# A four-layer graph network on one core: layer two's pass over all nodes dropped, its rows finished in the pass over edges

## The chip, the cores and the metric

One core of a Trainium2 chip runs the whole program, one launch. The metric is the device time in microseconds (us) of that core; a run's time takes in the program's span and what lies around it. Engine names are those of the profile: PE (TensorE), DVE (VectorE), ACT (ScalarE), POOL (GpSimd), SP (the queue that issues most transfers).

## The reference, cut to what matters

50,000 nodes with 256 features, 25,000 edges sorted by destination `dst`. Four layers, each followed by a layer norm over the features; all in float32.

```python
x = _layernorm(x + _L0_gnn_ref(...))   # messages, matmul, batch norm, relu, matmul
x = _layernorm(x + _L1_gnn_ref(...))   # x, mean of edge features, u -> hidden 512 -> 256
x = _layernorm(x + _L2_gnn_ref(x, src, dst, L2_gnn_W, L2_gnn_attn_l, L2_gnn_attn_r))
x = _layernorm(x + _L3_gnn_ref(x, edge_index, L3_gnn_W, ...))

def _L2_gnn_ref(feat, src, dst, W, attn_l, attn_r):          # 8 heads of 32
    ft = (feat @ W).reshape(n, H, D)
    a1, a2 = einsum('nhd,hd->nh', ft, attn_l), einsum('nhd,hd->nh', ft, attn_r)
    e = leaky_relu(a1[src] + a2[dst], 0.2)
    ex = exp(e - segment_max(e, dst)[dst])
    alpha = ex / segment_sum(ex, dst)[dst]
    return elu(segment_sum(ft[src] * alpha, dst))

def _L3_gnn_ref(...):   # 4 heads of 64; the same attention, with a self-loop for each node
    ...
    return elu(out + bias) + x
```

A node that is no edge's destination gets a zero sum in layer two, so that its new row is the layer norm of its old row, which is normed already: the old row times one factor. At most 25,000 of the 50,000 nodes are a destination.

## The kernel before

Seven stages run one after the other, with a barrier between them (`barrier`, the `tick` memset at L234). `PHASES` lists five programs for each stage, one for each engine. Each engine runs its instructions in the order in which the code writes them; semaphores tie them together.

- **Stage 1** (`p1_*`) sums the messages of the edges into `tab0` and prepares weights and indices. **Stage 2** (`p2_*`) is the first matmul of layer nought over all nodes, with the statistics of the batch norm.
- **Stage 3** (`p3_*`, "the layer-one pass") takes 98 steps of 512 nodes (`NS = 98`, `J = 4` rows of each of 128 partitions). A step k: PE runs `hidden(k)` (L1044, L1048), `mmA(k+2)` (L1024), then the transposes of k+1 (L1031, L1038) between the four groups of `mmB(k)` (L1067). ACT runs `relu(k)` (L959: four instructions, each frees a bank of PSUM), `evac(k+1)`, `y(k+3)`. DVE runs `first(k+2)` and `second(k)`: sum, statistics and, after POOL's power (L794), the scaling at L799, twice for each step. POOL runs `lnA.rstd(k+2)`, `lnB.rstd(k)`, `xb(k+3)` (L891), `x1_b(k+2)` (L897), and four indirect stores of step k-1 (L917). `mmA(k+3)` and `mmB(k+1)` wait for the whole of `relu(k+1)`, since its last bank is shared and its rows are the operand:

```python
if BA + j // 2 == HB[KH - 1]:
    wait(pe, p3["hidr"], KH * (k.s - 1))
```

- **Stage 4** (`edge_pass(2, ...)`, "layer two's edge pass") takes 49 steps of 512 edges. POOL gathers the source rows (L1181, four of a step) and scatters finished rows to `tab` (L1192, four). PE transposes and multiplies, DVE runs the segmented maximum and sum as scans, then for each of four tiles the recurrence L1387, L1391 and the division L1402.
- **Stage 5** (`node_pass`, "layer two's node pass") reads `tab` and `x2_d` for all nodes, takes the elu, the sum and the layer norm, stores `x3_d`, multiplies by layer three's weights and stores `h3_d` and the attention terms `ad_d`.
- **Stage 6** (`edge_pass(3, ...)`) does for layer three what stage 4 does for two, on rows of `h3_d` that need no matmul.
- **Stage 7** (`last_pass`) reads `tab`, `h3_d` and `x3_d` for all nodes: POOL multiplies two sets of rows (L1819), PE adds them, ACT and DVE take the elu and the norm.

## Time and profile before

| what | value |
|---|---|
| runs (3) | 5734.33, 5746.14, 5750.26 us; median 5746.14 |
| span of the profiled execution | 5581.5 us |
| busy in it: PE / DVE / ACT / POOL | 4162.6 / 3702.1 / 1962.3 / 3611.4 us |
| moved over HBM | 627.40 MB read, 543.83 MB written |

The profile shows one execution's span, from the first to the last instruction of the program; of that execution only the span is given. The runs' times are longer than a span, since they take in what lies around it: 5746.14 - 5581.5 = 164.6 us between the median and this span.

### The profile page before, as it was taken

What the parts mean: (1) busy time and instruction counts of PE and PEld (TensorE: products, weight loads), DVE (VectorE), ACT (ScalarE), POOL (GpSimd) and SP (SyncE); (2) the same over time, 40 slices, a digit from 0 to 9 for tenths busy, and PEclk for the clock granted to TensorE, in tenths of its full rate; (3) what the DMA queues carried; (4) which work ended last, traced back from release to release, by engine and by line L of the source; (5) the groups of instructions that cost most, each with busy time, mean ns of one, the idle gap of its engine ahead of it and who ended that gap; (6) DMA issues with size and microseconds to landing.
All of it is one profiled execution on the core that took longest, in us unless ns stands there. A gap on an engine that the chain in (4) does not pass through costs nothing. (4 is left out here: it accounts for less than half of the span.)

```text
span 5581.5 us, 69994 instructions
## 1 busy us (share of the span) xinstructions
PE 4162.6 (75%) x16758; PEld 2810.8 (50%) x16758; DVE 3702.1 (66%) x10203; ACT 1962.3 (35%) x3345; POOL 3611.4 (65%) x3319
## 2 busy tenths in 40 slices
PE   2276679999999999999999977776877500036666
PEld 1154445556666666666666667665666400012222
DVE  2155456666666666666666667777999665568887
ACT  0011135532222222222222222226888400026666
POOL 7488654443555556555555567775888777768887
PEclk7689889999999999999999988887999855569988
DMA  9988789985433333333333244447999733359998
GB/s 376 294 153 156 148 263 366 364 329 186 149 124 120 119 127 123 120 117 124 122 117 116 84 133 138 138 136 255 351 348 351 248 95 94 95 181 343 357 344 289
DMA packets 497175, 1129.62 MB, mean 202 GB/s; under 512 B 164007, under 2 KB 246907, under 8 KB 497031
## 3 DMA queue, kind: packets, MB, share of 16 engines
q1 hardware_dynamic: 331530, 866.20, 44.4%
q0 software_dynamic: 113184, 174.84, 12.9%
q10 hardware_dynamic: 52316, 87.06, 4.5%
q8 instruction: 41, 0.67, 0.0%
q14 instruction: 104, 0.84, 0.0%
HBM read 627.40 MB, written 543.83 MB: 210 GB/s over the span
## 5 line engine op out<-in xcount | busy, mean ns | idle before, releaser
L1067 PE MATMUL psum<-W2b,arena 128*128 128x256 f32 x3136 | 725.4, 380 | 0.0
L799 DVE TENSOR_SCALAR arena<-arena 128x256 f32<-128x256 f32 x784 | 462.6, 651 | 366.3 <-POOL arena L794 361.8
L1048 PE MATMUL psum<-arena,W1b 128*128 128x512 f32 x1568 | 699.2, 599 | 0.0
L1067 PEld LDWEIGHTS psum<-W2b,arena 128*128 128x128 f32 x3136 | 574.6, 191 | 65.2 <-issue 0.5
L1761 PE MATMUL psum<-arena,ident 128*128 128x512 f32 x784 | 409.9, 672 | 208.1 <-POOL arena L1819 206.0
L959 ACT ACTIVATE arena<-psum,hbias 128x512 f32<-128x512 f32 x392 | 269.4, 687 | 821.2 <-PE psum L1048 821.2
L1048 PEld LDWEIGHTS psum<-arena,W1b 128*128 128x128 f32 x1568 | 290.6, 190 | 401.7 <-issue 401.7
L1192 POOL DMA_INDIRECT tab<-arena,IDX x392 | 405.1, 1033 | 122.8 <-issue 91.5
L790 POOL TENSOR_TENSOR arena<-arena,lneps 128x4 f32<-128x4 f32 x196 | 41.5, 212 | 670.1 <-DVE arena L786 669.1
L1610 POOL DMA_INDIRECT ad_d<-arena,FE x392 | 394.6, 1007 | 114.3 <-issue 113.7
L917 POOL DMA_INDIRECT xd_d<-arena,FE x360 | 378.1, 1050 | 99.8 <-issue 96.9
L440 POOL DMA_INDIRECT tab<-arena x196 | 310.6, 1585 | 165.7 <-DMA tab<-zero 65.3
L1251 PE MATMUL psum<-ident,arena 128*128 128x128 f32 x24 | 5.8, 434 | 528.0 <-DVE arena L1419 516.8
L1555 PE MATMUL psum<-Wg,arena 128*128 128x264 f32 x1568 | 382.6, 400 | 19.2 <-DVE arena L1629 19.2
L1761 PEld LDWEIGHTS psum<-arena,ident 128*128 128x128 f32 x784 | 159.3, 213 | 458.0 <-issue 404.5
L1819 POOL TENSOR_TENSOR arena<-arena 128x1024 f32<-128x1024 f32 x196 | 368.3, 1900 | 10.4 <-DVE arena L1872 7.7
L1024 PE MATMUL psum<-W2a,arena 128*128 128x256 f32 x1568 | 356.9, 381 | 9.3 <-ACT arena L945 9.3
L752 PE MATMUL psum<-arena,W1a 128*128 128x512 f32 x784 | 353.7, 595 | 0.0
L702 POOL DMA_INDIRECT fe_d<-EID,FIRST x196 | 198.9, 1015 | 235.5 <-ACT arena L727 198.5
L1024 PEld LDWEIGHTS psum<-W2a,arena 128*128 128x128 f32 x1568 | 300.3, 192 | 91.6 <-issue 54.2
L1555 PEld LDWEIGHTS psum<-Wg,arena 128*128 128x128 f32 x1568 | 301.5, 197 | 76.2 <-DVE arena L1629 26.3
L577 PE MATMUL psum<-arena,NEG 128*128 128x324 f32 x500 | 161.2, 484 | 232.8 <-ACT arena L388 200.3
(256 smaller groups left out, 9286.1 us busy)
## 6 DMA issues: line engine op xcount, KB each, us to landing
arena<-tab SPq DMA_DIRECT2D x194, 544.0 KB
arena<-x_d SPq DMA_DIRECT2D x202, 512.0 KB, 7.0
arena<-in_x SPq DMA_DIRECT2D x194, 512.0 KB, 4.8
x_d<-arena SPq DMA_DIRECT2D x194, 512.0 KB, 2.9
tab<-zero SPq DMA_DIRECT2D x11, 5832.0 KB, 54.9
tab<-blank SPq DMA_DIRECT2D x97, 544.0 KB
h_d<-arena SPq DMA_DIRECT2D x97, 528.0 KB, 6.0
arena<-h_d SPq DMA_DIRECT2D x97, 528.0 KB, 5.5
```

Of the source, the lines that this page charges most:

```text
L440: pool.indirect_dma_start(out=tab0[:, :], out_offset=bass.IndirectOffsetOnAxis(ap=sidx[:, s, j:j + 1], axis=0), in_=comb[:, s % NC, j, :], ...
L752: last = pe.matmul(psum[:, 4 + 2 * b + g, :], W1a[:, f, g * P:(g + 1) * P], hT[:, b, f, :], start=(f == 0), stop=(f == FH - 1))
L799: v.tensor_scalar(y[:, j, :], r[:, j, :], self.mv[:, j, 0:1], self.rs[:, j:j + 1], ALU.subtract, ALU.mult).then_inc(self.s["y"], 1)
L917: pool.indirect_dma_start(out=xd_d[:, :], out_offset=bass.IndirectOffsetOnAxis(ap=FE[:, s * J + j:s * J + j + 1], axis=0), in_=x2[:, s % 2 ...
L1024: last = pe.matmul(outA(j), p3y[:, f, j * P:(j + 1) * P], W2a[:, f, :], start=(f == 0), stop=(f == FH - 1))
L1048: last = pe.matmul(psum[:, HB[c], :], W1b[:, f, c * P:(c + 1) * P], x1T[:, f, :], start=False, stop=(f == FH - 1))
L1067: last = pe.matmul(outB(j), hid[:, c, j * P:(j + 1) * P], W2b[:, c, :], start=(c == 0), stop=(c == KH - 1))
L1192: pool.indirect_dma_start(out=tab[:, :], out_offset=bass.IndirectOffsetOnAxis(ap=IDX[:, 2, c:c + 1], axis=0), in_=fin[:, s % NG, j, :], in ...
L1555: last = pe.matmul(psum[:, 2 + j, 0:HW], xT[:, k.slot(2), f, j * P:(j + 1) * P], Wg[3][:, f, :], start=(f == 0), stop=(f == FH - 1))
L1610: pool.indirect_dma_start(out=ad_d[:, :], out_offset=bass.IndirectOffsetOnAxis(ap=FE[:, c:c + 1], axis=0), in_=hs[:, k.slot(NB), j, D + H3 ...
L1761: last = pe.matmul(psum[:, b + i, :], ident[:, :], a[:, k.slot(2), 2 * i:2 * i + 2, :].rearrange("p j d -> p (j d)"), start=(n == 0), stop ...
L1819: pool.tensor_tensor(out=a[:, b, :, :].rearrange("p j (h c) -> p j h c", h=H), in0=t[:, k.slot(NB), :, 0:D].rearrange("p j (h c) -> p j h ...
```

## The change

Stage 5 is dropped, and its work is put in four other places.

- **Stage 3** writes `x3_d` for every node as if it were no destination: POOL takes one more power a step (`lone_pow`), ACT one more scaling of the step's rows (`lone_rows`), DVE three small instructions, SP one more store of 512 KB.
- **Stage 4** (`e2_*`) finishes the destination rows. The coefficients are divided once by the sum, so that the recurrence gives finished rows and L1402 goes. ACT takes relu and exp of a step's rows (`relu_exp`), DVE the elu (`settle`), POOL adds the destination's old rows (`residual`), DVE takes the statistics behind the next step's row sums (`measured`), POOL the power (`rstd`), ACT scales (`normed`), POOL scatters to `x3_d`. Two plain stores a step keep the unfinished and the finished rows in edge order (`raw_d`, `xl_d`). DVE copies the old row along a segment (one more 256-wide instruction for each tile).
- **Stage 6** (`e3_*`) goes through the edges from the last to the first, gathers rows of `x3_d`, and multiplies them itself, as stage 4 does. The self-loop's term is one more in its scans. DVE adds the bias (`biased`).
- **Stage 7** (`l_*`) reads `tab` and `x3_d`, and multiplies the rows by layer three's weights itself. DVE multiplies the product by the self-loop's share, POOL adds the edges' part (`total`) and the old rows (`residual`).

The core of the diff:

```diff
@@ p3_gpsimd @@
+            def lone_pow(k):
+                pool.wait_ge(lonely["lvar"], 3 * (k.s + 1))
+                wait(pool, lonely["lrow"], J * (k.s - 1))
+                pool.tensor_tensor(out=lonec[:, k.b, :], in0=lonev[:, k.b, :], in1=expo[:, 0:J], op=ALU.pow).then_inc(lonely["lpow"], 1)
             for s in range(NS):
...
                 if s + 2 < NS:
                     x1_b(at(s + 2))
+                if s > 0:
+                    lone_pow(at(s - 1))
@@ p3_scalar @@
+            def lone_rows(k):
+                act.wait_ge(lonely["lpow"], k.s + 1)
+                act.wait_ge(lnB.s["y"], J * (k.s + 1))
+                wait(act, p3_w3[k.b], 16 * k.n)
+                for j in range(J):
+                    act.activation(x3d[:, k.b, j, :], x2[:, k.b, j, :], ACT.Identity, bias=zero[:, 0:1], scale=lonec[:, k.b, j:j + 1]).then_inc(lonely["lrow"], 1)
...
                 if live(k.plus(3), NS):
                     y(k.plus(3))
-            run_steps(act, NS, body, tail=3)
+                if not (k.known() and k.s == 0):
+                    lone_rows(k.plus(-1))
+            run_steps(act, NS, body, peel=4, tail=3)
@@ e2_gpsimd @@
+            for s in range(CS + 2):
+                for j in range(J):
+                    if s + AHEAD < CS:
+                        gather(s + AHEAD, j)
+                    if s >= 2:
+                        scatter(s - 2, j)
+                    if j == 0 and 1 <= s <= CS:
+                        residual(s - 1)
+                    if j == J - 1 and 1 <= s <= CS:
+                        rstd(s - 1, ve2, neg2, rs2[:, (s - 1) % 2, :], nm2[:, (s - 1) % 2, :], J * (s - 2))
@@ e2_scalar @@
+            for s in range(CS):
+                ex(s)
+                if s + 1 < CS:
+                    for j in range(J):
+                        ev(s + 1, j)
+                if s > 0:
+                    normed(s - 1)
+                tail(s)
+                wait(act, e2["S"], J * (s + 1))
+                relu_exp(s, row2[:, s % NG, :, 0:D], un2, s)
@@ e2_vector @@
+            for s in range(CS):
+                chain(s)
+                if s > 0:
+                    settle(s - 1)
+                sums_rows(s)
+                if s > 0:
+                    measured(s - 1)
@@ l_gpsimd @@
+            def body(k):
+                total(k)
+                if not (k.known() and k.s < 1):
+                    residual(k.plus(-1))
+                if not (k.known() and k.s < 2):
+                    rstd(k.plus(-2))
@@ l_vector @@
+            def body(k):
+                weighted(k)
+                if not (k.known() and k.s < 1):
+                    unit(k.plus(-1))
+                if not (k.known() and k.s < 2):
+                    stats(k.plus(-2))
-        PHASES.append(edge_pass(2, x2_d, H2))
-        PHASES.append(node_pass(x2_d, x3_d))
-        PHASES.append(edge_pass(3, h3_d, H3))
-        PHASES.append(last_pass(x3_d, out, H3))
+        PHASES.append((e2_sync, e2_scalar, e2_gpsimd, e2_vector, e2_tensor))
+        PHASES.append((e3_sync, e3_scalar, e3_gpsimd, e3_vector, e3_tensor))
+        PHASES.append((l_sync, l_scalar, l_gpsimd, l_vector, l_tensor))
```

How the instructions stand, with the semaphores that they wait for. First ACT in the layer-one pass, a step k near its end and the first of the next: `relu(k)`, `evac(k+1)`, `y(k+3)`, `relu(k+1)`, before

```order
L959 ACTIVATE arena<-psum,hbias 128x512 [waits p3_hidw,p3_mmB]
L959 ACTIVATE arena<-psum,hbias 128x512 [waits p3_hidw] x3
L951 ACTIVATE arena<-psum 128x512 [waits p3_tr] x2
L953 ACTIVATE arena<-psum 128x512 [waits p3_tr]
L945 ACTIVATE arena<-arena,bnB,bnA 128x512 [waits p3_mmA,p3_h1]
L945 ACTIVATE arena<-arena,bnB,bnA 128x512
L959 ACTIVATE arena<-psum,hbias 128x512 [waits p3_hidw,p3_mmB]
```

and with the change:

```order
L1006 ACTIVATE arena<-psum,hbias 128x512 [waits p3_hidw,p3_mmB]
L1006 ACTIVATE arena<-psum,hbias 128x512 [waits p3_hidw] x3
L998 ACTIVATE arena<-psum 128x512 [waits p3_tr] x2
L1000 ACTIVATE arena<-psum 128x512 [waits p3_tr]
L992 ACTIVATE arena<-arena,bnB,bnA 128x512 [waits p3_mmA,p3_h1]
L992 ACTIVATE arena<-arena,bnB,bnA 128x512
L1013 ACTIVATE arena<-arena,zero 128x256 [waits p3_w31,lnB_y,p3_lpow]
L1013 ACTIVATE arena<-arena,zero 128x256 x3
L1006 ACTIVATE arena<-psum,hbias 128x512 [waits p3_hidw,p3_mmB]
```

The scaling of step k-1's rows (L1013), which waits for POOL's `lone_pow(k-1)` (semaphore p3_lpow), now stands between `y(k+3)` and `relu(k+1)`.

Then POOL in the same pass: the powers of k+2 (lnA) and k (lnB), `xb(k+3)`, `x1_b(k+2)`, the stores of k-1, before

```order
L790 TENSOR_TENSOR arena<-arena,lneps 128x4 [waits lnA_mv]
L794 TENSOR_TENSOR arena<-arena,expo 128x4 [waits lnA_ve,lnA_y]
L790 TENSOR_TENSOR arena<-arena,lneps 128x4 [waits lnB_mv]
L794 TENSOR_TENSOR arena<-arena,expo 128x4 [waits lnB_ve,lnB_y]
L891 TENSOR_TENSOR arena<-arena,b2a 128x1024 [waits p3_x0]
L897 TENSOR_TENSOR arena<-arena,b2b 128x1024 [waits lnB_y,lnA_y]
L917 DMA xd_d<-arena,FE 25088x256 [waits lnB_y]
```

and with the change:

```order
L813 TENSOR_TENSOR arena<-arena,lneps 128x4 [waits lnA_mv]
L817 TENSOR_TENSOR arena<-arena,expo 128x4 [waits lnA_ve,lnA_y]
L813 TENSOR_TENSOR arena<-arena,lneps 128x4 [waits lnB_mv]
L817 TENSOR_TENSOR arena<-arena,expo 128x4 [waits lnB_ve,lnB_y]
L930 TENSOR_TENSOR arena<-arena,b2a 128x1024 [waits p3_x0]
L936 TENSOR_TENSOR arena<-arena,b2b 128x1024 [waits lnB_y,lnA_y]
L962 TENSOR_TENSOR arena<-arena,expo 128x4 [waits p3_lrow,p3_lvar]
L956 DMA xd_d<-arena,FE 25088x256 [waits lnB_y]
```

The new power of step k-1 (L962, p3_lpow's source) stands behind the power of step k and both additions.

Last ACT in layer two's edge pass, one step s, before

```order
L1274 ACTIVATE arena<-arena 128x16x4 [waits g_S,g_d]
L1269 ACTIVATE arena<-psum 128x512 [waits g_mm,g_tr]
L1281 ACTIVATE arena<-arena 128x2x4x8 [waits g_s3,g_s]
L1269 ACTIVATE arena<-psum 128x512 [waits g_mm,g_tr] x3
L1274 ACTIVATE arena<-arena 128x16x4 [waits g_S,g_d]
```

and with the change:

```order
L1412 ACTIVATE arena<-arena 128x16x4 [waits e2_cf,e2_d]
L1407 ACTIVATE arena<-psum 128x512 [waits p2_mm,p2_tr] x4
L1431 ACTIVATE arena<-arena 128x256 [waits s_xd1,table_in1,e2_nm]
L1431 ACTIVATE arena<-arena 128x256 x3
L1417 ACTIVATE arena<-arena 128x2x4x8 [waits rows_out2,e2_s]
L1422 ACTIVATE arena<-arena 128x1024 [waits e2_u,e2_S]
L1424 ACTIVATE arena<-arena 128x1024 [waits e2_mn]
```

Between one step's exp (L1412, semaphore e2_d) and the next now stand `normed(s-1)` (L1431, which waits for POOL's `rstd(s-1)`, semaphore e2_nm) and `relu_exp(s)` (L1422, L1424, which wait for DVE's rows of step s, e2_S).

## Rows read from the trace of the kernel before

**Rows 1.** Windows, one for each of the seven stages, in order of time:

```profile
core 0 of [0], span 5581.5 us
core 0: us, PE busy (x) PEld busy (x) DVE busy (x) ACT busy (x) POOL busy (x), PEclk, DMA share, GB/s
0.00:745.00 745.00, 383.88 (x1386) 270.38 (x1386) 293.54 (x1032) 74.24 (x203) 505.75 (x414) 0.79 0.86 216
745.00:1183.00 438.00, 425.97 (x1568) 232.14 (x1568) 260.03 (x305) 241.04 (x392) 199.94 (x199) 0.98 0.98 352
1183.00:3232.00 2049.00, 2028.10 (x8232) 1370.70 (x8232) 1362.45 (x3237) 582.57 (x882) 1109.60 (x982) 1.00 0.39 133
3232.00:3798.00 566.00, 425.12 (x2408) 382.87 (x2408) 407.83 (x1493) 140.01 (x297) 413.04 (x397) 0.82 0.43 134
3798.00:4434.00 636.00, 482.97 (x2352) 389.46 (x2352) 553.31 (x1470) 489.83 (x784) 487.65 (x441) 0.94 0.95 327
4434.00:4954.00 520.00, 6.74 (x28) 5.98 (x28) 300.99 (x1049) 29.68 (x150) 391.10 (x397) 0.50 0.33 102
4954.00:5581.00 627.00, 409.86 (x784) 159.26 (x784) 523.91 (x1617) 404.90 (x637) 504.37 (x492) 0.90 0.92 328
```

**Rows 2.** Timeline of PE, one step of the layer-one pass and the next's start:

```profile
...
2711.18 1.99 PE L1044 MATMUL psum<-arena,W1e 64*128 64x512 f32 x8
...
2720.07 3.62 PE L1024 MATMUL psum<-W2a,arena 128*128 128x256 f32 x16
...
2731.84 1.99 PE L1044 MATMUL psum<-arena,W1e 64*128 64x512 f32 x8
...
```

**Rows 3.** Timeline of ACT, the same step:

```profile
...
2735.78 0.69 ACT L959 ACTIVATE arena<-psum,hbias 128x512 f32<-128x512 f32 x1 [5.29 <-PE psum L1048]
...
```

**Rows 4.** Timeline of POOL, the same step:

```profile
...
2735.32 1.01 POOL L794 TENSOR_TENSOR arena<-arena,expo 128x4 f32<-128x4 f32 x1 [0.44 <-POOL arena L790]
...
2739.90 2.35 POOL L897 TENSOR_TENSOR arena<-arena,b2b 128x1024 f32<-128x1024 f32 x1 [1.26 <-DVE arena L799]
```

**Rows 5.** Timeline of DVE, the same step:

```profile
...
2736.36 3.40 DVE L799 TENSOR_SCALAR arena<-arena 128x256 f32<-128x256 f32 x4 [1.76 <-POOL arena L794]
...
```

**Rows 6.** DVE's product at L982: engine, count, duration ns min/median/max, first and last:

```profile
...
L982 DVE TENSOR_TENSOR arena<-arena x98: 693/2624/2725, 1189.8 to 3173.6; 128x512 f32<-128x512 f32 x98
...
```

**Rows 7.** Windows in layer two's edge pass, columns as in rows 1:

```profile
...
3455.80:3459.20 3.40, 0.00 (x0) 0.00 (x0) 3.26 (x10) 0.00 (x0) 2.48 (x4) 0.89 0.72 244
3459.30:3465.20 5.90, 5.90 (x20) 5.18 (x21) 2.47 (x17) 1.45 (x3) 4.66 (x5) 0.50 0.30 91
...
```

**Rows 8.** Groups by form, layer two's edge pass: busy us, mean ns | idle:

```profile
...
L1192 POOL DMA_INDIRECT tab<-arena,IDX x196 | 208.0, 1061 | 63.0 <-issue 56.1 <-ACT arena L1269 3.5 <-DVE arena L1402 1.8
...
```

**Rows 9.** Timeline of DVE, one step of layer two's edge pass:

```profile
...
3453.30 0.24 DVE L1320 TENSOR_TENSOR_SCAN arena<-arena 128x40 f32<-128x40 f32 x1 [0.32 <-ACT arena L1274]
...
3455.12 0.36 DVE L1387 TENSOR_TENSOR arena<-arena 128x256 f32<-128x256 f32 x1
...
3457.11 0.42 DVE L1387 TENSOR_TENSOR arena<-arena 128x256 f32<-128x256 f32 x1
...
3458.27 0.41 DVE L1387 TENSOR_TENSOR arena<-arena 128x256 f32<-128x256 f32 x1
...
```

**Rows 10.** Groups by form, last pass, columns as in rows 8:

```profile
...
L1819 POOL TENSOR_TENSOR arena<-arena 128x1024 f32<-128x1024 f32 x196 | 368.3, 1900 | 10.4 <-DVE arena L1872 7.7 <-PE psum L1761 2.7
L1787 ACT ACTIVATE arena<-arena 128x256 f32<-128x256 f32 x392 | 201.8, 585 | 2.9 <-POOL arena L1831 2.4 <-ACT arena L1787 0.5
L1890 DVE BATCH_NORM_STATS2 arena<-arena 128x6 f32<-128x256 f32 x392 | 137.7, 413 | 5.5
L1882 DVE SCALAR_TENSOR_TENSOR psum<-arena,psum 128x1024 f32<-128x1024 f32 x98 | 120.0, 1225 | 15.6 <-ACT arena L1780 10.6 <-issue 5.0
...
L1780 ACT ACTIVATE arena<-arena 128x1024 f32<-128x1024 f32 x98 | 103.6, 1057 | 3.1
...
L1894 DVE BATCH_NORM_AGGREGATE arena<-arena 128x2 f32<-128x6 f32 x392 | 36.6, 156 | 4.3
...
```

More of the change, by code:

```diff
@@ L821, in gnn_program @@
         p3_w = [sem(f"p3_w{b}") for b in range(2)]
+        p3_w3 = [sem(f"p3_w3{b}") for b in range(2)]
+        lonely = {k: sem(f"p3_{k}") for k in ("lvar", "lpow", "lrow")}
         p3_fill = sem("p3_fill")
@@ L878, in body @@
                     store(k.plus(-4))
+                if not (k.known() and k.s < 5):
+                    store3(k.plus(-5))
                 if k.known() and 12 <= k.s < 12 + LATE:
@@ L1091, in gnn_program @@
         PHASES.append((p3_sync, p3_scalar, p3_gpsimd, p3_vector, p3_tensor))
-        once = {k: sem(f"g_{k}") for k in ("zero", "end", "old", "spread", "top", "z2", "wx", "f0", "wT", "new", "fr", "row", "fix", "near")}
-        edge2 = {k: sem(f"g_{k}") for k in
-                 ("tr", "ev", "mm", "chain", "eL", "M", "d", "w", "s", "tail", "A", "B", "S", "head", "inv", "full")}
         NG = 4
-        gs = [sem(f"g_g{b}") for b in range(NG)]
-        sc = [sem(f"g_s{b}") for b in range(NG)]
@@ new lines, in gnn_program @@
+        zb2 = take([H2, P])
+        wT2 = take([H2, P])
+        mx2 = take([H2])
+        df2 = take([2, H2])
+        wf2 = take([2, H2])
+        sn2 = take([H2])
+        pick = take([P])
+        same0 = take([C])
+        few = take([6])
+        e2 = {k: Signal(sem(f"e2_{k}")) for k in
+              ("tab", "rowd", "zero", "head", "hrow", "ev", "chain", "eL", "M", "d", "w", "s", "tail", "cf", "B", "A", "S", "xc",
+               "mn", "ex", "u", "r", "nm", "end", "spread", "top", "wx", "wT", "old", "z", "wf", "new", "fix", "fixed")}
@@ new lines, in gnn_program @@
+        ws3 = take([2, H3, J + 1])
+        inv3 = take([H3, J])
+        cf3 = take([2, 2, H3, J + 1])
+        om3 = take([2, H3, J + 1])
+        endrow3 = take([TW])
+        oldrow3 = take([TW])
+        newrow3 = take([TW])
+        tO3 = take([TW])
+        zb3 = take([H3, P])
+        wT3 = take([H3, P])
+        mx3 = take([H3])
+        df3 = take([2, H3])
+        wf3 = take([2, H3])
+        sn3 = take([H3])
+        e3_end = cursor[0]
+        done2 = dict(zero=5, head=16, tr=J * CS, ev=J * CS, mm=J * CS, chain=CHAIN * CS, eL=3 * CS, M=2 * CS, d=2 * CS, w=CS, s=CS, tail=CS,
+                     cf=3 * CS, B=2 * CS, A=J * CS, S=J * CS, end=2, spread=3, top=3, wx=1, wT=1, old=16, z=2, wf=1, new=13, fix=1, fixed=32)
@@ new lines, in gnn_program, with l_rows, l_sync, tables @@
+        l_w = [e2_xl[b].after(16 * turns(b)) for b in range(NG)]
+        def l_rows(sp, k):
+            b = k.slot(NXT)
+            wait(sp, lp["r"], k.s - NXT + 1)
+            a, n = node_view(x3_d, k)
+            sp.dma_start(l_xt[0:n, b, :, :], a).then_inc(l_x[b].sem, 16)
+        def l_sync(sp):
+            def tables(k):
+                b = k.slot(NTT)
+                wait(sp, lp["t"], k.s - NTT + 1)
+                a, n = node_view(tab, k)
+                sp.dma_start(l_tt[0:n, b, :, :], a).then_inc(l_t[b].sem, 16)
+            for s in range(NTT):
+                tables(beat(s, PER))
+            def body(k):
+                if live(k.plus(NTT), NS):
+                    tables(k.plus(NTT))
+                if not (k.known() and k.s == 0) and live(k.plus(NXT - 1), NS):
+                    l_rows(sp, k.plus(NXT - 1))
+            run_beats(sp, NS, body, PER, tail=NXT)
+            for b in range(4):
+                wait(sp, l_w[b], 16 * ((NS + 3 - b) // 4))
```

1667 lines of the change are left out of this document (898 added, 769 removed).

## The prediction

> **What bounds the kernel now.** First the windows, one for each stage [rows 1], since a mean over the span mixes seven different limits. The reader is to see three kinds. Stages 2 and 3 are PE's: 2028.1 of 2049 us busy in stage 3, at a granted clock of 1.00. Stages 5 and 7 are the transfers': DMA share 0.95 and 0.92 at 327 and 328 GB/s, with no engine over 90% busy. Stages 4 and 6 are POOL's: each of its indirect requests takes 1.061 us and 63.0 / 196 = 0.32 before the next [rows 8], so eight of a step take 11.0, and 49 steps 541 of the stage's 566 us. Then the timelines of one step of stage 3, one for each engine [rows 2 to 5]. A step lasts 2731.84 - 2711.18 = 20.66 us, and PE never stands; the other engines have slack, but their order within the step is tight, and that is where this change puts its new instructions.
>
> **Stage 5, dropped.** Its whole window goes: -636 us [rows 1]. Its transfers need not be made up elsewhere: the 51 MB of `x3_d` are now stored in stage 3 (98 steps of 512 KB), where the DMA share is 0.39.
>
> **Stage 3: one factor and one scaling a step.** By busy time this is free: ACT is busy 582.6 of 2049 us and POOL 1109.6 [rows 1]. By order it is not. `lone_rows(k-1)` stands on ACT ahead of `relu(k+1)`, and waits for `lone_pow(k-1)`, which stands on POOL behind `x1_b(k+2)`. That in turn waits for DVE's scaling in `second(k)`, which comes after `mmB(k)`. So `relu(k+1)`, due at 2735.78 [rows 3], falls behind all of these. Step by step, with `mmB(k)` ending at 2731.84 [rows 2]:
> DVE's scaling ends at 2736.36 + 3.40 = 2739.8 [rows 5], and about 0.4 later with three small instructions between (my estimate, below the 0.24 each of a scan over 40 columns [rows 9]): 2740.2. `x1_b` takes 2.35 [rows 4]: 2742.6. The power takes 1.01 [rows 4] and a signal: 2743.7. Four scalings of 256 columns at 0.585 [rows 10]: 2746.0. Four relus at 0.69 [rows 3]: 2748.8. Only now may PE take the second half of `mmA(k+3)`, 3.62 / 2 = 1.8 us [rows 2], and then the transposes and `mmB(k+1)`, which last 2731.84 - (2720.07 + 3.62) = 8.15 [rows 2]: 2758.8. From one end of `mmB` to the next that is 27.0 us, 6.3 more than 20.66, and it is a closed loop: the next step starts with the same delay. PE stands from the half of `mmA`, 2740.7 + 1.8 = 2742.5, to 2748.8, in one piece.
>
> Such a standstill has a second price. In stage 4 PE stood for the 3.4 us from 3455.8, and then worked for 5.9 us without a gap at a granted clock of 0.50, the lower level of 1.2 GHz [rows 7]. If the 6.3 us do the same, the work behind them begins at 1.2 GHz, and it is all on the loop. Bounds: nothing, or 3.0 us, half of those 5.9; I take 2.3, since part of the low stretch falls into the standstill. The Trainium skill ("TensorE: Matmul & The Clock Gate", Part 1) says that the throttled state is the default and that activity releases it, with no third level between; by that rule the clock falls in each step, and the trace agrees, with 0.50 and 1.00.
> So a step takes 27.0 + 2.3 = 29.3, and 96 steps have both neighbours: 96 x 8.6 = **+826 us** (bounds 96 x 6.3 = 605 and 96 x 9.3 = 893).
>
> **Stage 4: rows finished.** Again the order decides, not the sum. Let DVE's row sums of step s end at 0. `measured(s-1)`: four statistics and four aggregates, 4 x 0.413 + 4 x 0.156 [rows 10], 2.3. POOL's power and product, 1.01 [rows 4] and 0.2 (estimate): 3.5. ACT's `normed(s-1)`, 4 x 0.585 [rows 10]: 5.8; its copy of the sums, 0.3 (estimate): 6.1; `relu_exp(s)`, 2 x 1.057 [rows 10]: 8.3. DVE, which has long done `chain(s+1)`, has waited for that; `settle(s)` takes what L1882 takes, 1.22 [rows 10]: 9.5. Then `sums_rows(s+1)`: from the scan to the first row product it is 3455.12 - 3453.30 = 1.8 now [rows 9], and 2.3 with the two small products more; for each tile three 256-wide instructions, as now (the old row's copy where the division was), 3458.27 - 3457.11 = 1.16 [rows 9], so 4.6.
> Between them comes a new collision: POOL adds the destination rows, 1024 columns from two tiles of SBUF, just when DVE has small products with two operands there. The row to read is L982: 0.693 us at the least, 2.624 at the median [rows 6], and in each step `x1_b` runs at that moment (2739.90 to 2742.25 [rows 4]). So DVE's product waits for POOL's addition to end. I take 2.35 as its length, since it is an addition of the same shape as `x1_b`; the other bound is the 1.90 of L1819 [rows 10], a product with a broadcast. Of the 2.3 us of small work at most the scan and the reciprocal run beside it or before it (0.35, an estimate): +2.0. The loop is 9.5 + 2.3 + 4.6 + 2.0 = 18.4 us; without the collision and with the short addition 16.4; with the six requests between `residual` and `rstd` at 1.38 each as the longer way, up to 19.5. The Trainium skill ("SBUF — State Buffer", "Who interferes with whom") has the rule for this: VectorE with two SBUF inputs and GpSimd reading SBUF exclude each other for a whole instruction. By it the loop is 18.4, without it 16.4, a difference of 98 us in the stage; rows 6 agree with it. For the addition's length only a page has a figure of the plain kind ("GPSIMD Engine Reference", 3.1): 4497 ns for 2048 columns, so an estimate of 2.25 for 1024, which would take 5 us off the stage.
> 49 x 18.4 = 902, and 40 for filling and for the last row's repair (now 566 - 541 = 25, plus one step's lag): 942 against 566, **+376 us** (bounds +278, +430).
>
> **Stage 6: its own matmul, backwards.** POOL's eight requests a step stay, and with them the stage's step now, 520 / 49 = 10.6 [rows 1]. DVE: stage 4's 407.8 / 49 = 8.3 now [rows 1], less four divisions (each a third of the 1.16 in rows 9, so 1.5), plus a bias addition of 1.2 [rows 10] and a dozen small ones (1.8, an estimate): 9.8. PE's part, absent now, needs a bank that DVE frees shortly before the row sums end, and may be late by 1 us at the lower clock (an estimate). I take 11.5: 49 x 11.5 + 30 = 594, **+74 us** (bounds 10.6 and 12.5 a step: +29, +123).
>
> **Stage 7: a quarter fewer bytes.** 512 + 544 + 512 KB in place of 2096 a step: at 328 GB/s [rows 1] 4.9 us, so the transfers no longer bind (6.4 a step now). POOL does: two additions of 1024 columns, 2 x 2.35, and 1.2 for power and product, with gaps 6.1; and DVE's `unit`, 1.22, also reads two SBUF tiles, so that it excludes the additions: 7.3 if it never falls beside the power, 6.1 if always. I take 6.7: 98 x 6.7 + 15 = 672 against 627, **+45 us** (bounds 5.3, with additions of 1.90 and no exclusion, so -90; 7.3, so +104). Stages 1 and 2 keep their work but for a few instructions (0 us).
>
> **Sum.** -636 + 826 + 376 + 74 + 45 = +685 on the profiled span: 5581.5 + 685 = 6266. The median of the runs is 164.6 above that span, and what lies around a span does not change: 6431, so 6430 us.
>
> **Rivals.**
> - *The standstill without the clock's fall.* For: in stages 5 and 7 PE stands 1.6 and 2.2 us in each of 98 steps, and the clock is still 0.94 and 0.90 [rows 1]. Against: rows 7. 6430 - 96 x 2.3 = 6209. Chance 0.17.
> - *Stage 4 keeps to POOL's own pace*, 11.0 + 2.35 + 1.2 = 14.6 a step, the other engines' loop being shorter than I read it. For: POOL binds there now. Against: the loop has each link in the code. 6430 - 49 x 3.8 = 6244. Chance 0.08.
> - *The scaled rows do hide in stage 3* (the other side). For: ACT and POOL have over 900 us each to spare there. Against: the order of rows 4 and 3, with `relu(k+1)` due at 2735.78 and `x1_b` beginning at 2739.90. 6430 - 826 = 5604, faster. It decides where the delay is below 1.5 us a step, since the rest sums to -141 us and 141 / 96 = 1.5. Chance 0.10.
> - *Nothing to tell*: gains and losses cancel to within 0.3% (17 us, about what a measurement here can tell). Chance 0.03.
> - My forecast, with both prices in stage 3: 0.62, its own range 6250 to 6640.
>
> Slower is 0.62 + 0.17 + 0.08 = 0.87. All low bounds together give 5930 and all high ones 6660; they are independent, so I take 6050 to 6640, which holds the first two rivals and leaves out the third, the fourth and the corners.
>
> **What would show it.** In stage 3: steps of 27 to 29 us in place of 20.66, PE idle once a step for about 6 us before L1024's counterpart or the relus' reader, released by ACT; ACT's `lone_rows` released by POOL's power; a granted clock below 0.9. In stage 4: DVE idle ahead of `settle`, released by ACT's exp, about 3.5 us a step, and a median near 2 us for the coefficient product. In stage 7: DMA share near 0.75 and POOL over 85% busy. I am wrong if `x1_b(k+2)` runs ahead of the scaling of step k, or if stage 3 stays near 2049 us.

## The result, and the profile after

The changed kernel takes 6399.28 us, median of 4 runs (6394.61 to 6409.17), the kernel before 5746.53 in the same comparison: ratio 1.1137, 95% interval 1.1119 to 1.1154. That is 653 us more; the prediction said 6430, within 6050 to 6640. The number is right to 0.5%, but it is a sum in which two errors of some 165 us cancel (a stage mis-sized, and a difference between two executions taken for a constant); they are taken apart below.

The windows of the changed kernel, one for each stage in order of time (stage 5 is gone, so these are stages 1, 2, 3, 4, 6, 7), to be read against [rows 1]:

```profile
core 0: us, PE busy (x) PEld busy (x) DVE busy (x) ACT busy (x) POOL busy (x), PEclk, DMA share, GB/s
0.00:745.50 745.50, 406.39 (x1386) 280.62 (x1386) 292.95 (x1032) 73.91 (x203) 506.15 (x414) 0.76 0.86 215
745.50:1187.10 441.60, 426.47 (x1568) 231.73 (x1568) 259.87 (x305) 240.71 (x392) 199.21 (x200) 0.98 0.98 349
1187.10:4014.50 2827.40, 2277.32 (x8232) 1520.56 (x8232) 1379.44 (x3531) 741.84 (x1274) 1222.12 (x1081) 0.89 0.33 114
4014.50:4944.10 929.60, 486.07 (x2410) 424.48 (x2410) 665.54 (x2163) 326.41 (x593) 595.86 (x547) 0.69 0.40 135
4944.10:5705.60 761.50, 481.57 (x2388) 423.69 (x2388) 436.69 (x1942) 128.37 (x297) 392.19 (x397) 0.73 0.32 102
5705.60:6385.20 679.60, 508.80 (x2352) 424.47 (x2352) 519.07 (x1274) 503.82 (x780) 650.82 (x394) 0.90 0.68 224
```

In stages 3, 4 and 6, which grew most, no engine is busy for more than 0.81 of the window and the DMA share is 0.40 or less: something waits for something, in each. Stage 3 alone is 778 us longer.

Stage 3 against [rows 2 to 4]: first ACT's timeline around one standstill (start, length, what, and in brackets the idle time before it and what ended it):

```profile
3109.24 2.07 ACT L1013 ACTIVATE arena<-arena,zero 128x256 f32<-128x256 f32 x4 [13.34 <-POOL arena L962]
3111.21 2.39 ACT L1006 ACTIVATE arena<-psum,hbias 128x512 f32<-128x512 f32 x4
```

POOL's timeline, just before it:

```profile
3105.35 2.35 POOL L936 TENSOR_TENSOR arena<-arena,b2b 128x1024 f32<-128x1024 f32 x1 [1.60 <-DVE arena L1075]
3107.66 1.46 POOL L962 TENSOR_TENSOR arena<-arena,expo 128x4 f32<-128x4 f32 x1
```

And PE's:

```profile
3106.13 1.89 PE L1094 MATMUL psum<-W2a,arena 128*128 128x256 f32 x8
3113.65 3.78 PE L1094 MATMUL psum<-W2a,arena 128*128 128x256 f32 x8 [5.63 <-ACT arena L1006]
```

This is the predicted loop link by link: DVE's scaling (L1075), `x1_b` (L936), the lone rows' power (L962), the lone rows (L1013), the relus (L1006), and only then PE. ACT has stood for 13.34 us before its lone rows. PE stands 5.63 us, and its second eight products last 3.78 us, twice the 1.89 of the first eight: the granted clock is 0.50 from 3113.65 to 3117.40, the lower of the clock's two levels, 1.2 GHz, after the standstill.

Stage 4, DVE and POOL in one step, against [rows 9]. Settle waits for the exponential; beside POOL's addition (L1311) DVE's product of 64 columns takes 1.94 us:

```profile
4517.85 1.22 DVE L1537 SCALAR_TENSOR_TENSOR arena<-arena 128x1024 f32<-128x1024 f32 x1 [4.21 <-ACT arena L1424]
...
4519.15 2.34 POOL L1311 TENSOR_TENSOR arena<-arena 128x1024 f32<-128x1024 f32 x1 [3.18 <-DVE arena L1537]
...
4519.64 1.94 DVE L1565 TENSOR_TENSOR arena<-arena 128x64 f32<-128x64 f32 x1
```

Stage 6, groups of instructions over the whole stage (count, busy us, mean ns, idle us before them and who ended it; "remote" stands where the profile shows no instruction behind the signal). This stage's loop I had not worked out:

```profile
L1761 PE MATMUL psum<-Wg,arena 128*128 128x260 f32 x784 | 287.5, 503 | 250.5 <-ACT arena L1798 250.5
L1721 POOL DMA_INDIRECT tab<-arena,IDX x196 | 198.2, 1011 | 288.1 <-DVE arena L1878 229.0 <-issue 58.8 <-ACT arena L1808 0.3
...
L1837 DVE SCALAR_TENSOR_TENSOR arena<-KEEP,psum 128x8 f32<-128x8 f32 x98 | 15.9, 163 | 288.3 <-remote 263.7 <-PE psum L1763 21.4 <-issue 3.3
...
L1803 ACT ACTIVATE arena<-arena 128x48 f32<-128x48 f32 x49 | 11.9, 243 | 337.4 <-DVE arena L1872 337.4
```

Every engine waits for another one: PE for ACT's copies, ACT for DVE's chain, POOL for DVE's biased rows, and DVE, at the second instruction of its chain, for PE's last products. Lines of one step from the timelines of DVE, ACT and PE, in order of time:

```profile
5311.96 0.16 DVE L1837 SCALAR_TENSOR_TENSOR arena<-KEEP,psum 128x8 f32<-128x8 f32 x1 [4.89 <-remote]
...
5314.17 0.24 ACT L1803 ACTIVATE arena<-arena 128x48 f32<-128x48 f32 x1 [7.14 <-DVE arena L1872]
5314.32 1.06 ACT L1798 ACTIVATE arena<-psum 128x512 f32<-128x512 f32 x2
5314.95 2.10 PE L1761 MATMUL psum<-Wg,arena 128*128 128x260 f32 x4 [5.30 <-ACT arena L1798]
...
5324.20 0.51 PE L1763 MATMUL psum<-Wg,arena 128*128 128x8 f32 x4
...
5327.50 0.17 DVE L1837 SCALAR_TENSOR_TENSOR arena<-KEEP,psum 128x8 f32<-128x8 f32 x1 [6.26 <-remote]
```

This is the stage's loop. In the mean over the steps it takes 2.2 us from DVE's L1837 to ACT's exponential (L1803), 0.8 from there to PE's first product, 9.1 for PE's four times 128 rows with their copies, and 2.6 from the end of PE's last record to DVE's next L1837: 14.7 us, 49 times 720 of the stage's 762.

### The profile page after: what moved, and what is told of

The parts are those of the page before. It is cut to its first block and busy times, and to the rows that moved or that the text cites. A ratio compares the mean times of both kernels' runs of the same rounds, so it can differ in the third digit from the quotient of the medians.

```text
span 6395.2 us, 70077 instructions
## 1 busy us (share of the span) xinstructions
PE 4586.6 (72%) x18336; PEld 3305.5 (52%) x18336; DVE 3553.6 (56%) x10247; ACT 2017.3 (32%) x3543; POOL 3566.4 (56%) x3029
## 5 line engine op out<-in xcount | busy, mean ns | idle before, releaser
L1094 PE MATMUL psum<-W2a,arena 128*128 128x256 f32 x1568 | 546.1, 510 | 534.2 <-ACT arena L1006 524.8
L1094 PEld LDWEIGHTS psum<-W2a,arena 128*128 128x128 f32 x1568 | 392.3, 258 | 686.2 <-ACT arena L1006 562.6
L1013 ACT ACTIVATE arena<-arena,zero 128x256 f32<-128x256 f32 x392 | 203.0, 588 | 1281.7 <-POOL arena L962 1281.7
L1044 DVE TENSOR_TENSOR arena<-psum,arena 128x512 f32<-128x512 f32 x196 | 134.5, 686 | 813.3 <-PE psum L1094 813.3
L1372 PE MATMUL psum<-Wg,arena 128*128 128x264 f32 x784 | 289.6, 506 | 385.3 <-ACT arena L1407 383.6
L2030 PE MATMUL psum<-Wg,arena 128*128 128x256 f32 x1568 | 423.1, 431 | 153.5 <-ACT arena L2048 153.5
L1761 PE MATMUL psum<-Wg,arena 128*128 128x260 f32 x784 | 287.5, 503 | 250.5 <-ACT arena L1798 250.5
L2030 PEld LDWEIGHTS psum<-Wg,arena 128*128 128x128 f32 x1568 | 331.6, 216 | 227.7 <-ACT arena L2048 154.5
L1372 PEld LDWEIGHTS psum<-Wg,arena 128*128 128x128 f32 x784 | 179.1, 253 | 422.5 <-ACT arena L1407 395.4
L1721 POOL DMA_INDIRECT tab<-arena,IDX x196 | 198.2, 1011 | 288.1 <-DVE arena L1878 229.0
L1761 PEld LDWEIGHTS psum<-Wg,arena 128*128 128x128 f32 x784 | 180.6, 255 | 286.1 <-ACT arena L1798 262.7
L936 POOL TENSOR_TENSOR arena<-arena,b2b 128x1024 f32<-128x1024 f32 x98 | 230.1, 2348 | 157.0 <-DVE arena L1075 154.0
```

The costliest lines, as they stand in the source:

```text
L936: pool.tensor_tensor(out=x1b[:, k.b, :, :], in0=x1[:, k.b, :, :], in1=b2b[:, :].rearrange("p (a d) -> p a d", a=1).to_broadcast([P, J, D]) ...
L1013: act.activation(x3d[:, k.b, j, :], x2[:, k.b, j, :], ACT.Identity, bias=zero[:, 0:1], scale=lonec[:, k.b, j:j + 1]).then_inc(lonely["lrow ...
L1094: last = pe.matmul(outA(j), p3y[:, f, j * P:(j + 1) * P], W2a[:, f, :], start=(f == 0), stop=(f == FH - 1))
L1372: pe.matmul(o[:, 0:D + H2], xT2[:, j % 2, f, :], Wg[2][:, f, 0:D + H2], start=(f == 0), stop=(f == FH - 1))
L1721: pool.indirect_dma_start(out=tab[:, :], out_offset=bass.IndirectOffsetOnAxis(ap=IDX[:, 3, c:c + 1], axis=0), in_=fin3[:, s % NG, i, :], i ...
L1761: pe.matmul(o[:, 0:D + H3], xT3[:, i % 2, f, :], Wg[3][:, f, 0:D + H3], start=(f == 0), stop=(f == FH - 1))
```

## The experiments

Stage lengths below are read between the barrier's marks, each from one profiled execution; "us" is the median of four or more runs, but of one run for `e0_before` and `e10_tensor_less`. The kernel before was timed beside each.

| run | us | stage 3 | 4 | 5 | 6 | 7 |
|---|---|---|---|---|---|---|
| before, first profile | 5746.53, its runs | 2049 | 566 | 637 | 520 | 619 |
| before, second profile (`e0_before`) | 5762.88 | 2048 | 630 | 667 | 594 | 626 |
| changed | 6399.28 | 2827 | 930 | - | 762 | 680 |
| `e1_pow_first` | 5648.22 | 2063 | 938 | - | 766 | 680 |
| `e2_ev_first` | 6367.15 | 2825 | 929 | - | 736 | 679 |
| `e3_exp_first` | 6282.64 | 2828 | 811 | - | 767 | 680 |
| `e13_stats_first` | 6373.80 | 2827 | 907 | - | 759 | 680 |
| `e9_tiny_loads` | 6403.77 | 2830 | 929 | - | 765 | 679 |
| `e5_exp_dve_adds` | 6206.64 | 2838 | 731 | - | 759 | 680 |
| `e6_all_orders` | 5485.31 | 2063 | 811 | - | 734 | 682 |
| `e8_orders_dve` | 5513.47 | 2071 | 732 | - | 726 | 794 |
| `e11_orders_dve4` | 5411.70 | 2069 | 730 | - | 742 | 679 |
| `e10_tensor_less` | 5315.20 | 2067 | 732 | - | 640 | 682 |
| `e12_scatter_later` | 5298.84 | 2066 | 731 | - | 618 | 681 |

**What the profile of before was.**

> The kernel before, unchanged, profiled a second time. The changed kernel's run is 2.5 us longer than its span (6397.69 against 6395.2); before's profiled span lies 164.6 us under the median of its runs. Theory: nothing of 165 us lies around a span; before's profiled execution was itself some 160 us shorter than its other runs. Then this run's span is 2 to 3 us under its own time, and that time is either again near 5584 or near 5746; in the second case some stage of it is longer than in the first profile, and says which (744.5, 438.8, 2048.7, 565.6, 636.7, 519.7, 618.6 us there). Rival, as the prediction had it: the span is again near 5582 and the time near 5746.

Its span is 5761.2 us, under a time of 5762.88: nothing of 165 us lies around a span, and the first profile showed an execution quicker than any timed run. Stages 1 to 3 agree to 3 us; stages 4, 5, 6 and 7 are 65, 30, 74 and 8 longer. The windows of stages 4, 5 and 6 in the second profile, against [rows 1]:

```profile
3234.90:3865.30 630.40, 467.70 (x2408) 409.33 (x2408) 408.92 (x1493) 136.53 (x297) 405.14 (x396) 0.78 0.38 120
3865.30:4532.40 667.10, 493.01 (x2352) 395.66 (x2352) 551.54 (x1470) 492.87 (x784) 484.39 (x442) 0.93 0.90 312
4532.40:5126.10 593.70, 6.74 (x28) 5.99 (x28) 305.69 (x1049) 29.70 (x150) 391.09 (x397) 0.50 0.29 89
```

DVE's, ACT's and POOL's busy times are those of the first profile within 3%, so what grew is mostly waiting; PE is busy 43 us longer in stage 4, at a granted clock of 0.78 for 0.82. One place of stage 6 shows which waiting. DVE's timeline in the second profile:

```profile
4803.03 0.18 DVE L1352 TENSOR_TENSOR arena<-arena 128x16 f32<-128x16 f32 x1 [3.30 <-remote]
4804.43 0.18 DVE L1354 SCALAR_TENSOR_TENSOR arena<-arena 128x16 f32<-128x16 f32 x1 [1.22 <-DVE arena L1352]
4805.83 0.20 DVE L1320 TENSOR_TENSOR_SCAN arena<-NEG,arena 128x20 f32<-128x20 f32 x1 [1.22 <-DVE arena L1354]
4807.23 0.18 DVE L1359 TENSOR_TENSOR arena<-arena 128x16 f32<-128x16 f32 x1 [1.20 <-DVE arena L1320]
```

The same four operations in the first profile, DVE's timeline:

```profile
4700.64 0.18 DVE L1352 TENSOR_TENSOR arena<-arena 128x16 f32<-128x16 f32 x1 [3.87 <-DMA arena<-h_d,IDX]
4700.85 0.17 DVE L1354 SCALAR_TENSOR_TENSOR arena<-arena 128x16 f32<-128x16 f32 x1
4701.06 0.20 DVE L1320 TENSOR_TENSOR_SCAN arena<-NEG,arena 128x20 f32<-128x20 f32 x1
4701.30 0.17 DVE L1359 TENSOR_TENSOR arena<-arena 128x16 f32<-128x16 f32 x1
```

Each operation waits for the semaphore of the one just ahead of it on its own engine. In the first profile the signal is there at once, in the second it takes 1.2 us here. Over stage 6, such waits of DVE for itself alone are over 0.3 us in 69 of 301 cases, 76 us together, and never in the first profile (0.06 us at the most): about the 74 us by which the stage is longer. In stage 4 PE's signals are late. ACT's copies there, first profile, then second:

```profile
L1269 ACT ACTIVATE arena<-psum 128x512 f32<-128x512 f32 x196 | 116.7, 596 | 370.5 <-PE psum L1226 369.4
L1269 ACT ACTIVATE arena<-psum 128x512 f32<-128x512 f32 x196 | 113.2, 596 | 452.9 <-remote 152.3 <-PE psum L1226 139.0 <-PE psum L1237 84.4
```

Counted from the end of PE's records that a copy waits for (or of ACT's own last instruction, if that is later), 55 of 195 copies start over 0.5 us late, 188 us together; in the first profile none does. The 30 us of stage 5, where the transfers fall from 327 to 312 GB/s, are not traced to anything. So signals came late in stages 4 and 6, and the timed runs of before, at 5734 to 5770 us, are as long as this second execution. Why they are late is open; a candidate is the recording itself, though the first execution was recorded too. The second trace holds 49,859 semaphore updates where the first holds 80,775. The Trainium skill ("NOTIFIC — the notification-queue block", 7.1) says that the block that takes the records never loses one inside but holds its producers up; no run here tested that.

**Stage 3: order or work.**

```diff
             for s in range(NS):
+                if s > 0:
+                    lone_pow(at(s - 1))
                 if s + 2 < NS:
                     lnA.rstd(pool, at(s + 2))
...
-                if s > 0:
-                    lone_pow(at(s - 1))
                 if LATE < s < NS - 1:
```

> The changed kernel with one edit: GpSimd does the lone rows' power of step s-1 first in its pass s, ahead of both root steps, instead of last, behind the rows' add. Nothing is left out. Theory (stage 3's loss is ScalarE waiting with the lone rows for a power that GpSimd does behind work which itself waits for this step's VectorE, so a wait that closes a loop, and not work): stage 3 falls from 2827 to about 2050 to 2130 us, ScalarE's wait at the lone rows from 13.3 us a step to under 3, the granted clock there from 0.89 to near 0.99; the whole falls by some 700 to 780 us, to about 5620 to 5700 us. Rival (the step is longer by its added work: 2.07 us of ScalarE, 1.02 of GpSimd, VectorE's small products and the added store): the order is worth little and stage 3 stays over 2650 us.

```profile
1185.20:3247.70 2062.50, 2029.24 (x8232) 1368.22 (x8232) 1367.72 (x3531) 763.02 (x1274) 1211.65 (x1081) 1.00 0.47 157
```

5648.22 us, 0.9827 of before (0.9806 to 0.9848): one instruction in another place is worth 751 us, and the kernel is 1.7% faster than before in place of 11% slower. PE is busy as before the change, at a clock of 1.00, and all the added work of the lone rows costs 14 us. One number was off: ACT still waits 409.4 / 98 = 4.2 us at the lone rows, not under 3, but nothing is late behind it.

**Stage 4: the order on ACT, and who adds.**

```diff
-                if s > 0:
-                    normed(s - 1)
                 tail(s)
                 wait(act, e2["S"], J * (s + 1))
                 relu_exp(s, row2[:, s % NG, :, 0:D], un2, s)
+                if s > 0:
+                    normed(s - 1)
```

> The changed kernel with one edit in stage 4 (layer two's edge pass): ScalarE does the relu and the exponential of rows s ahead of the normed rows s-1, instead of behind them. Nothing is left out. Theory (the loop of stage 4 is VectorE's statistics s-1, GpSimd's power, ScalarE's normed rows s-1, relu and exponential s, VectorE's settle s, its row sums, statistics s): VectorE's wait of 4.0 to 4.2 us at settle goes, the step falls from 17.94 to 13.7 to 14.5 us, stage 4 from 930 to 720 to 780 us. Rival (GpSimd's add locks VectorE out and GpSimd's own 11.5 us a step with its waits set the pace): VectorE's wait moves to GpSimd's sum and the step stays over 16.5 us.

811 us, from 930: the wait at settle is gone, as the theory had it, but the stage is 31 us above the theory's range, at 15.4 us a step, between the theory and its rival. DVE, now without a gap there, runs into POOL's addition with its next operation, the scan of the row sums. That group in `e3_exp_first`:

```profile
L1195 DVE TENSOR_TENSOR_SCAN arena<-arena 128x40 f32<-128x40 f32 x49 | 121.0, 2470 | 40.8 <-ACT arena L1412 40.8
```

The next run keeps this edit and takes the addition away from POOL (its `residual` goes, DVE does the same behind settle):

```diff
             def settle(s):
...
+                wait(v, e2["u"], s + 1)
+                wait(v, e2["xc"], J * s + J - 1)
+                v.tensor_tensor(out=rr2[:, b, :, :], in0=xd2[:, c, :, :], in1=rr2[:, b, :, :], op=ALU.add).then_inc(e2["r"].sem, 1)
```

> The kernel of e3_exp_first with one more edit in stage 4: the destination rows are added by VectorE right behind its settle, and not by GpSimd. Nothing is left out. Behind e3_exp_first VectorE is busy nearly without a gap, and its small scan beside GpSimd's add of 2.37 us takes 2.74 us in place of 0.23. Theory (VectorE sets the pace there, and GpSimd's add costs it 2.5 us a step by holding it up, against some 1.2 us for doing the add itself): stage 4 falls from 811 to 725 to 760 us, the small operation behind settle is back under 0.4 us. Rival (moving work onto the engine that sets the pace costs it what the add takes, 1.2 to 2.4 us a step): stage 4 rises to 850 us or more.

731 us, as the theory had it. DVE does the addition in 1.23 us, and its scan is back at 274 ns:

```profile
L1538 DVE TENSOR_TENSOR arena<-arena 128x1024 f32<-128x1024 f32 x49 | 60.0, 1225 | 1.7
...
L1195 DVE TENSOR_TENSOR_SCAN arena<-arena 128x40 f32<-128x40 f32 x49 | 13.4, 274 | 0.3 <-issue 0.3
```

The change also puts the statistics behind the row sums. That part undone, with DVE's `measured(s - 1)` ahead of `sums_rows(s)`:

```diff
                     settle(s - 1)
+                    measured(s - 1)
                 sums_rows(s)
-                if s > 0:
-                    measured(s - 1)
```

> The changed kernel with one edit in stage 4: VectorE takes the statistics of rows s-1 ahead of the row sums of tile s, where the change puts them behind. Nothing is left out. Theory (in the changed kernel statistics, power, normed rows, relu, exponential and settle form one loop of 17.94 us a step; ahead of the row sums they run beside them): VectorE waits some 3 us for GpSimd's add and saves the 4.2 us at settle and 1.7 us of the held-up product; the step falls to 15.5 to 17 us, stage 4 from 930 to 800 to 880 us. Rival (the wait for GpSimd's add comes on top, the wait at settle stays): 20 us or more a step, stage 4 over 1000 us.

907 us, 22 less: the right sign, and too small for the theory; the rival's 1000 is far off. The timeline of one step, DVE and POOL, shows why:

```profile
4504.65 1.23 DVE L1537 SCALAR_TENSOR_TENSOR arena<-arena 128x1024 f32<-128x1024 f32 x1 [3.05 <-ACT arena L1424]
...
4508.33 1.40 DVE L1544 BATCH_NORM_STATS2 arena<-arena 128x6 f32<-128x256 f32 x4 [2.46 <-POOL arena L1311]
...
4510.26 0.16 DVE L1553 TENSOR_SCALAR arena<-arena 128x4 f32<-128x4 f32 x1
...
4516.21 1.23 POOL L1316 TENSOR_TENSOR arena<-arena,expo 128x4 f32<-128x4 f32 x1
```

The statistics are ready at 4510.42, but POOL takes their power at 4516.21, behind its six requests. Settle still waits, 3.05 us here. The loop keeps its links and only changes the one that is late.

**Stage 6: copies, loads, TensorE, requests.**

```diff
             for s in range(CS):
+                if s + 1 < CS:
+                    for i in range(2):
+                        ev(s + 1, i)
                 ex(s)
                 if s + 1 < CS:
-                    for i in range(J):
+                    for i in range(2, J):
                         ev(s + 1, i)
```

> The changed kernel with one edit in stage 6 (layer three's edge pass): ScalarE does the first two copies of tile s+1 for TensorE ahead of the exponential of tile s, which waits for VectorE's chain. Nothing is left out. Theory (the term of stage 6 was sized too small because its loop is chain(s), exponential, four copies, four tiles of TensorE at half clock for the first two, chain(s+1)): two tiles of TensorE's work go under the chain, the step falls from 14.6 to about 11 to 12 us, stage 6 from 761 to 580 to 640 us, VectorE's wait at its second copy out of PSUM from 4.9 to 6.3 us to under 2. Rival (the stage is longer because the transfers or GpSimd's requests limit it: 8 requests of 1.3 us are 10.4 us a step): it stays within 20 us of 761.

736 us, 26 less than 762, neither theory's number (the rival's bound was 20). This does not show that the order of copies and exponential is a small part, for the edit brings late signals with it. ACT's copies of stage 6 in the changed kernel, then in this run:

```profile
L1798 ACT ACTIVATE arena<-psum 128x512 f32<-128x512 f32 x196 | 110.8, 590 | 279.0 <-PE psum L1763 168.3 <-PE psum L1752 87.1 <-issue 15.7
L1798 ACT ACTIVATE arena<-psum 128x512 f32<-128x512 f32 x196 | 116.6, 596 | 502.3 <-remote 271.3 <-PE psum L1752 219.4 <-issue 9.9
```

Counted as above, 2 of 195 copies start over 0.5 us late in the changed kernel (9 us together) and 60 of 195 here (322 us).

```diff
+                elif s < NG:
                     sp.dma_start(xd3[:, s % NG, :, :], slots[CS - 1 - s, :, :, :]).then_inc(e3_gd[s % NG].sem, 16)
+                else:
+                    sp.dma_start(xd3[:, s % NG, :, 0:8], slots[CS - 1 - s, :, :, 0:8]).then_inc(e3_gd[s % NG].sem, 16)
```

> The changed kernel, where stage 6 loads 8 of the 256 columns of each destination row from its fifth tile on (the rest keeps what earlier tiles left, so this part of the computation is left out); the number of transfers and of their signals stays. In the changed kernel TensorE's last copy of a tile is over at 5309.17 us by the records, and VectorE, which waits for it, goes on at 5311.96. Theory (the 512 KB load that is under way at that moment, 5307 to 5309, holds up TensorE's work or its signals): stage 6 falls from 761 to 620 to 680 us and VectorE's wait of 4.9 to 6.3 us to under 3. Rival (the late signals come by themselves or from the indirect transfers, as they do in the second profile of the kernel before, whose stage 6 has no such load and is still 74 us longer than in the first): stage 6 stays over 730 us.

765 us: the bytes of these loads have no part in it, the theory falls.

The three orders together, and then with DVE's additions:

> The changed kernel with the three edits of order together (e1_pow_first, e2_ev_first, e3_exp_first); nothing is left out. Theory (three separate loops in three stages, their gains add): 6399 - 751 - 32 - 117 = 5499, so 5480 to 5520 us, some 4% under the kernel before. Rival (they share a cause, such as the clock or the late signals): the gains do not add, 5550 us or more.

5485.31 us, 0.9550 of before (0.9527 to 0.9573): the gains add, as separate loops' gains do.

```diff
             def unit(k):
...
+                v.tensor_tensor(out=l_ex[:, b, :, :], in0=l_ex[:, b, :, :], in1=l_xt[:, k.slot(NXT), :, :], op=ALU.add).then_inc(lp["r"].sem, 1)
```

> The kernel of e6_all_orders with the destination rows of stage 4 added by VectorE (as in e5_exp_dve_adds) and the rows of x3 in stage 7 added by VectorE right behind its unit step, where GpSimd is busy 650.8 of 679.6 us. Nothing is left out. Theory (GpSimd bounds stage 7 and its adds hold VectorE up): stage 7 falls from 680 to 580 to 620 us, stage 4 to 725 to 760; the whole comes to 5340 to 5400 us. Rival (stage 7 is bound by its 224 GB/s of transfers, share 0.68): stage 7 falls by under 20 us.

Stage 4 did as told, stage 7 went the other way, from 680 to 794 us, which neither theory had. Groups of stage 7 in this run:

```profile
L2137 DVE TENSOR_TENSOR arena<-arena 128x1024 f32<-128x1024 f32 x98 | 328.9, 3356 | 3.3
...
L2097 POOL TENSOR_TENSOR arena<-arena 128x1024 f32<-128x1024 f32 x98 | 240.1, 2450 | 19.5 <-DVE arena L2126 19.5
```

The addition that took DVE 1.225 us in stage 4 takes 3.356 here, since POOL's other addition (2.45 us) runs at the same time. In the step looked at they start together, at 5109.78 and 5109.76, and DVE's ends 1.1 us behind POOL's, about its own length alone: DVE stands for POOL and then works. DVE is then busy 750.6 of 793.5 us. Without that edit:

> The kernel of e6_all_orders with the destination rows of stage 4 added by VectorE (as in e5_exp_dve_adds), and stage 7 as in the changed kernel. Nothing is left out. Theory (the four edits act in separate stages, so their gains add): 5485 us less the 80 us that e5_exp_dve_adds took off stage 4, so 5395 to 5415 us, about 0.941 of the kernel before. Rival (stage 4's gain is given back in the next stages): 5450 us or more.

5411.70 us, 0.9408 (0.9385 to 0.9430), as expected to 0.1%. On this base come the last two runs. The first leaves part of stage 6's computation out, as its expectation says:

```diff
-                for n, a in enumerate((xs3[:, s % NG, i, :], xd3[:, s % NG, J - 1 - i, :])):
+                for n, a in enumerate((xs3[:, s % NG, i, :], xd3[:, s % NG, J - 1 - i, :])[0:2 if s < 2 else 1]):
...
-                for f in range(FH):
+                for f in range(FH if s < 2 else 0):
                     done = pe.matmul(o[:, D + H3:D + 3 * H3], ...
```

> The kernel of e11_orders_dve4, where stage 6 from its third tile on leaves out the destination rows' two transposes and two small products per 128 rows (the values of earlier tiles stay in their place, so this part of the computation is left out): 8 of TensorE's 16 instructions per 128 rows less, its copies on ScalarE unchanged. Theory (TensorE's own work, as late as its signals come, is in the loop that sets stage 6): the step falls by the time of what is left out, 0.96 us per 128 rows at full clock and 1.9 at half, so by 4 to 7 us of 14.9, stage 6 from 734 to 510 to 600 us, where GpSimd's requests (10.4 us a step) end it. Rival (the stage is bound by requests, transfers or signals): it stays over 690 us.

640 us against 742: between the two theories. TensorE's part is in the loop, but half of its products and transposes (by the records 6 of 12 for each 128 rows) are worth 2 us a step and not 4 to 7.

```diff
-            for s in range(CS + 2):
+            for s in range(CS + 3):
...
-                    if s >= 2:
-                        scatter(s - 2, i)
+                    if s >= 3:
+                        scatter(s - 3, i)
```

> The kernel of e11_orders_dve4 with one edit in stage 6: GpSimd scatters finished rows one step later (tile s-3 in step s in place of s-2), so that it hardly waits for VectorE's biased rows (in the changed kernel 229 us of waits there) and issues its gathers earlier. Nothing is left out. Theory (late gathers are what holds TensorE's transposes, GpSimd's queue being part of the loop): stage 6 falls from 734 to 600 to 660 us. Rival (GpSimd's wait is only the echo of a loop between VectorE, ScalarE and TensorE): stage 6 stays within 20 us of 734.

618 us against 742, in the theory's range; the whole takes 5298.84 us, 0.9218 of before (0.9193 to 0.9243), the fastest kernel of this study. The group of POOL's scatters in stage 6 of `e11_orders_dve4`:

```profile
L1722 POOL DMA_INDIRECT tab<-arena,IDX x196 | 206.5, 1054 | 225.3 <-DVE arena L1882 167.6 <-issue 57.3 <-ACT arena L1809 0.3
```

The same group of `e12_scatter_later`:

```profile
L1722 POOL DMA_INDIRECT tab<-arena,IDX x196 | 207.7, 1060 | 87.5 <-issue 63.4 <-DVE arena L1882 23.5 <-ACT arena L1809 0.6
```

POOL's wait for DVE's rows falls by 144 us and the stage by 124. So the place of the scatter is worth 124 us; but it does not work by late gathers, as I had put it. PE's transposes wait as little for gathers before the edit as behind it, once, where the stage begins:

```profile
L1753 PE MATMUL psum<-ident,arena 128*128 128x128 f32 x784 | 148.1, 321 | 21.0 <-DMA arena<-x_d,IDX 21.0
L1753 PE MATMUL psum<-ident,arena 128*128 128x128 f32 x784 | 145.5, 316 | 21.3 <-DMA arena<-x_d,IDX 21.3
```

What does fall is the lateness of signals behind PE's records: of ACT's copies from 322 to 210 us, of DVE's L1841 (the changed kernel's L1837) from 114 to 19. Why later scatters let PE's signals come sooner is open.

## Why the prediction was right, and where it was wrong

- **Stage 5 dropped (-636).** Right; against the second profile it is -667.
- **Stage 3 (+826).** Right in each link, and 48 us too long. PE's idle time there is 524.8 us behind the relus, 5.4 a step where I had 6.3; PE's busy time is 2277.3 - 2029.2 = 248 us above that of `e1_pow_first`, so the clock's fall costs 2.5 a step (I had 2.3, within 0 to 3.0). The rival without the clock's fall is refuted by 3.78 against 1.89 us, the one in which the rows hide by the 13.34 us of ACT's wait. It would have been true with the power in another place: `e1_pow_first` is that rival, at 5648 us against its 5604.
- **Stage 4 (+376, to 942 us).** Right. The loop of 18.4 us is 17.85 in the trace (settle to settle, in the mean), the stage 930. Settle waits 3.9 us in the mean, where I had 3.5, and the product beside POOL's addition takes 1.90, so that the collision costs 1.7 a step where I had 2.0. The rival of 14.6 us a step is wrong here, though `e5_exp_dve_adds` gets close to it.
- **Stage 6 (+74, to 594 us).** This is the term that was mis-sized: 762 us. The step that failed is "PE's part ... may be late by 1 us ... I take 11.5". I had added up each engine's work, and not walked the loop as for stages 3 and 4. PE's part does not run beside DVE's chain but in one loop with it: the chain waits for PE's fourth 128 rows, these for ACT's copies, the copies stand behind the exponential of the tile before, and that waits for the chain. In place of 11.5 us a step the loop takes 14.7: 2.2 for the chain, 0.8 for exponential and first copy, 9.1 for PE's part at a granted clock of 0.73 over the stage, and 2.6 until DVE goes on. Without the last link it would be 12.1, near my upper bound of 12.5; so up to 132 of the 168 us that are missing are late signals: 45 of 98 of DVE's L1837 start over 0.5 us after the end of PE's records, which is modelled. ACT goes on at once behind PE in the same stage (2 of 195 copies are late), as in stage 4. What makes DVE's signals late is open. POOL's wait for DVE's biased rows (229 us, 4.7 a step) is no link of this loop: its gathers run three tiles ahead, and PE's transposes wait for one only where the stage begins (21.1 us). Even so a scatter one step later takes 124 us away in `e12_scatter_later`, where fewer signals are late; the copies' order takes 26.
- **Stage 7 (+45, to 672 us).** Right: 680, POOL busy 650.8 of it; the DMA share is 0.68 where I had 0.75. My lower bound for it comes to -93 by the sum given, not -90.
- **The sum.** The step "what lies around a span does not change" (164.6 us) was wrong: that difference was no constant around a span, but the first profile's quicker execution. The changed kernel's time is 2.5 us above its span. Stage 6 was 168 us too short, the others together 39 too long; with the 165 added for the wrong reason the sum is 31 too high. The number was right by that chance; the side and the size came from stage 3, which was right by its own steps.
- Against the second profile of before, which is as long as the timed runs, the change is +779 (stage 3), +299 (4), -667 (5), +168 (6) and +53 (7), in all +634 between spans 5761.2 and 6395.2. On this footing my +685 is 51 too high: stage 6 is 94 too short, stages 3, 4 and 5 are 47, 77 and 31 too high, stage 7 is 8 too short. Even this is no equal footing in each stage, since stage 4 has late signals in that execution of before and hardly any in the changed kernel.
